# Loads, weight transposes, weight rounding and tables moved into the stages in front of them, in a four-layer network on one core

## The reference, cut to what matters

```
x  = x + attn0(xn) + ffn0(xn)   # causal softmax attention with ALiBi; quantised SiLU feed-forward
x  = x + attn1(xn) + ffn1(xn)   # linear attention with cos/sin features and decay; quantised feed-forward
x  = x + attn2(xn) + ffn2(xn)   # attention with relative position tables; a two-layer local-attention network
x  = x + attn3(xn) + ffn3(xn)   # attention with tied q, k, v; mixture of 8 experts, top 2

def fp4_quant_dequant(x):       # blocks of 16 along the last axis, for activations and for weights
    scale = max(max|x| / 6, 1e-12)
    return nearest_of(0, .5, 1, 1.5, 2, 3, 4, 6)(|x / scale|) * sign(x) * scale
```

## Time and profile before

| what | value |
|---|---|
| median of three runs | 4258.23 us |
| the profiled execution, its own time | 4260.68 us |
| its span | 4258.7 us |
| busy: TensorE, VectorE, ScalarE, GpSimd | 2931.0, 2349.2, 1746.5, 826.7 us |
| granted TensorE clock, mean | 0.783 |

### The profile page before, as it was taken

One profiled execution on the slowest core, in us unless ns is written; L12 is line 12 of the kernel. 1 busy time (PEld: TensorE's weight loads), 2 busy tenths in 40 slices (PEclk: granted clock), 3 DMA queues, 4 the chain that ended last, 5 costly groups with the idle time before them and its releaser, 6 DMA issues. The chain is left out here.

```text
span 4258.7 us, 67695 instructions
## 1 busy us (share of the span) xinstructions
PE 2931.0 (69%) x21547; PEld 1596.1 (37%) x21547; DVE 2349.2 (55%) x4792; ACT 1746.5 (41%) x4244; POOL 826.7 (19%) x1061
## 2 busy tenths in 40 slices
PE   5588846374635787777776687777778722768885
PEld 2344424253423444444443343333333311762221
DVE  4556467454855566666663354444445453138885
ACT  2355511211213455455553244444444401227775
POOL 2100001021113444444441300000000004112220
PEclk9789867686767999999998666666666655889998
DMA  3432110000001000000000577777777615663331
GB/s 113 79 56 52 38 53 0 8 1 6 1 14 48 10 19 18 18 10 18 18 18 3 170 189 196 187 192 192 187 193 192 161 42 158 174 146 55 66 61 37
DMA packets 462309, 340.77 MB, mean 80 GB/s; under 512 B 64351, under 2 KB 424986, under 8 KB 461986
## 3 DMA queue, kind: packets, MB, share of 16 engines
q1 hardware_dynamic: 441474, 308.78, 29.4%
q0 software_dynamic: 8704, 20.99, 1.8%
q10 hardware_dynamic: 11808, 7.08, 0.6%
HBM read 174.71 MB, written 146.81 MB: 75 GB/s over the span
## 5 line engine op out<-in xcount | busy, mean ns | idle before, releaser
L1158 DVE TENSOR_REDUCE a_soft_NM<-a_soft_s_ps 128x2 f32<-128x1024 f32 (+3 forms) x512 | 514.2, 1021 | 204.3 <-PE a_soft_s_ps L1093 132.8
L1192 ACT ACTIVATE a_soft_PTS<-a_soft_st_ps 128x512 f32<-128x512 f32 (+3 forms) x1024 | 458.3, 521 | 147.9 <-PE a_soft_st_ps L1069 101.7
L465 PE MATMUL a_soft_pt_ps<-net_ident,a_soft_PR 128*128 128x128 f32 x1280 | 330.1, 370 | 123.2 <-ACT a_soft_PTS L567 115.8
L613 ACT ACTIVATE a_soft_PR<-a_soft_s_ps,a_soft_least 128x128 f32<-128x128 f32 (+3 forms) x512 | 263.9, 527 | 338.7 <-DVE a_soft_least L588 241.8
L1064 PE MATMUL a_soft_st_ps<-a_soft_QS,a_soft_KS 50*128 50x512 bf16 (+4 forms) x1024 | 257.8, 359 | 60.1 <-ACT a_soft_PTS L1192 32.2
L465 PEld LDWEIGHTS a_soft_pt_ps<-net_ident,a_soft_PR 128*128 128x128 f32 x1280 | 184.1, 181 | 220.8 <-ACT a_soft_PR L613 160.0
L1106 PE MATMUL a_soft_o_ps<-a_soft_PTS,a_soft_VR 128*32 128x512 f32 (+3 forms) x2048 | 240.9, 544 | 0.1
L2275 PE MATMUL f_run_ps<-f_run_WQKV,f_run_HT 128*128 128x512 f32 x384 | 228.9, 687 | 15.2 <-DVE f_run_RS L1496 8.0
L2608 ACT ACTIVATE f_run_PB<-f_run_ps,f_run_MX 128x128 f32<-128x128 f32 x512 | 180.3, 378 | 134.0 <-DVE f_run_MX L2490 134.0
L2413 POOL TENSOR_TENSOR f_run_QK<-f_run_QK,f_run_T 128x512 f32<-128x512 f32 x128 | 163.4, 1277 | 365.6 <-DVE f_run_T L2468 363.2
L569 DVE COPY a_soft_PTS<-a_soft_pt_ps 128x512 f32<-128x512 f32 (+3 forms) x320 | 169.5, 530 | 72.6 <-PE a_soft_pt_ps L465 40.0
(11 more groups left out here) (382 smaller groups left out, 6395.5 us busy)
## 6 DMA issues: line engine op xcount, KB each, us to landing
a_soft_BIAS<-skew_d SPq DMA_DIRECT2D x256, 191.0 KB, 4.3
band_d<-a_soft_PR SPq DMA_DIRECT2D x256, 191.0 KB, 3.8
skew_d<-a_soft_RS SPq DMA_DIRECT2D x128, 256.0 KB, 4.5
a_soft_PB<-band_d SPq DMA_DIRECT2D x128, 256.0 KB, 3.1
f_run_W<-in_L_ffn_w SPq DMA_DIRECT2D x72, 256.0 KB, 2.7
query_rows_d<-a_proj_PARTS SPq DMA_DIRECT2D x96, 128.0 KB, 3.4
key_rows_d<-a_proj_PARTS SPq DMA_DIRECT2D x96, 128.0 KB, 3.8
a_soft_QS<-query_rows_d SPq DMA_DIRECT2D x32, 384.0 KB
```

Of the source, the lines that this page charges most:

```text
L465: last = pe.transpose(pt_ps[:, slot, kb * P:(kb + 1) * P], PR[:, n % NPR, OFF + kb * P:OFF + (kb + 1) * P], ident[:])
L613: act.activation(PR[:, n % NPR, OFF:OFF + width(j)], s_ps[:, n % 4, 0:width(j)], ACT.Exp, bias=least[:, n:n + 1], scale=-1.0).then_inc(pro ...
L1158: dve.tensor_reduce(NM[:, T % 2, j, p, :], s_ps[:, ring["s", a] % 2, :, 0:width(j)], AX.X, ALU.max, negate=True).then_inc(max_ready, 1)
L1192: act.activation(PTS[:, T % 2, 2 * p + par, kb, q0:S], st_ps[:, e % 3, q0:S], ACT.Exp, scale=scale).then_inc(probs_ready, 1)
```

## The change

Preparation is taken out of stages of its own. What it does:

- x is loaded in eight pieces inside n0, with the statistics of each piece behind its load; the identity, a0's weights, masks and biases, the relative tables' rows and the raw weights of both quantised feed-forwards are loaded behind x in the same stage (40 loads). `layernorm_stage` gets loads, transposes (TensorE, ScalarE, in front of the square root) and a first piece of GpSimd work (in front of its copies).
- The six weight matrices are rounded on VectorE inside the attention a0, one of ten instructions every fourth step. `fp4_weights` is gone; the nine blocks of a feed-forward are turned at the start of its own run.
- In f0 the tables of a1 are loaded and the angles computed on GpSimd between batches; the sines and exponentials are made by ScalarE in n1, which also turns a1's weights. GpSimd splits and stacks the relative keys there, with DMAs from its own queue.
- In f1 the weights and tables of f2 are loaded; GpSimd scales the rotary tables between batches. The shift and gain of f2 move to step 14 of its order.
- a2 loads its four weights and two small tables in one stage; n3 takes over the loads, casts and transposes of the last layer.
- The ALiBi rows are written to the query and key tiles from SBUF and no longer through DRAM.

```diff
-def layernorm_stage(nc, stage, X, XN, XNT, ident):
+def layernorm_stage(nc, stage, X, XN, XNT, ident, fill=(), loads=(), turns=(), first_pool=None, first_act=None):
+        @block.sync
+        def _(sp):
+            for b, src in enumerate(fill):
+                sp.dma_start(X[:, TB * b:TB * (b + 1), :], src).then_inc(x_loaded[b], 16)
+            for dst, src in loads:
+                sp.dma_start(dst, src).then_inc(loaded, 16)
+            if loads:
+                sp.wait_ge(loaded, 16 * len(loads))
...
+            for b in range(len(fill)):
+                dve.wait_ge(x_loaded[b], 16)
+                for t in range(TB * b, TB * (b + 1)):
+                    dve.bn_stats(st[:, t, :], X[:, t, :])
...
         @block.scalar
         def _(act):
+            if first_act is not None:
+                first_act(act)
+            for k, (dst, src) in enumerate(turns):
+                a, b = src.shape
+                act.wait_ge(w_turned, k + 1)
+                act.activation(dst, w_ps[0:b, k % 2, 0:a], ACT.Copy).then_inc(w_copied, 1)
             act.wait_ge(var_ready, 1)
             act.activation(rstd[:], var[:], ACT.Sqrt).then_inc(sd_ready, 1)
...
         @block.gpsimd
         def _(pool):
+            if first_pool is not None:
+                if loads:
+                    pool.wait_ge(loaded, 16 * len(loads))
+                first_pool(pool, stored)
             pool.sem_inc(xn_copied, 1)
...
         @block.tensor
         def _(pe):
+            if loads and turns:
+                pe.wait_ge(loaded, 16 * len(loads))
+            for k, (dst, src) in enumerate(turns):
+                ...
+                pe.transpose(w_ps[0:b, k % 2, 0:a], src, ident[0:a, 0:a]).then_inc(w_turned, 1)
...
# turned_attention, VectorE, behind the maxima of a step
+                if matrices and t >= 8 and t % 4 == 0 and (t - 8) // 4 < FP4_STEPS * len(matrices):
+                    dve.drain()
+                    fp4_step(dve, (t - 8) // 4 % FP4_STEPS, matrices[(t - 8) // 4 // FP4_STEPS], QSC[:], QINV[:], QT[:], QM[:])
...
# fp4_ffn, GpSimd
             for b in range(B):
+                if b == 1:
+                    pool.wait_ge(loaded, 16 * len(loads))
+                if b >= 1:
+                    between(pool, b)
                 pool.wait_ge(h_rounded, b + 1)
                 pool.tensor_tensor(HH[:, b % 2, :]..., t[:, b % 2, :]..., bcast(sc[:, b % 2, :], FP4_BLOCK), ALU.mult)
...
# fp4_ffn, TensorE, ahead of turn_x(0)
+            for n in range(3):
+                out = ht_ps[:, n, :] if n < 2 else y_ps[:]
+                for c in range(3):
+                    last = pe.transpose(out[:, c * P:(c + 1) * P], RAW[:, n, c * P:(c + 1) * P], ident[:])
+                last.then_inc(w_turned, 1)
...
+    def angles(self, pool, b):                    # f0, between batches, 128x1024 each
+        if b == 1:
+            for g in range(2):
+                pool.tensor_scalar(ang[:, g, :], self.t["tok_idx"][:], self.t["th"][:, g:g + 1], None, ALU.mult)
+            pool.drain()
+            pool.tensor_scalar(kk[:], ang[:], float(1 / (2 * np.pi)), quarter[:, 0:1], ALU.mult, ALU.add)
+        elif b == 2:
+            pool.tensor_scalar(kk[:], kk[:], ROUND, None, ALU.add)
+            pool.drain()
+            pool.tensor_scalar(kk[:], kk[:], ROUND, None, ALU.subtract)
+        elif b <= 5:
+            step = self.t["TRIG"]
+            pool.tensor_scalar(step[:], kk[:], -TWO_PI[b - 3], None, ALU.mult)
+            pool.drain()
+            pool.tensor_tensor(ang[:], step[:], ang[:], ALU.add)
+        elif b == 6:
+            pool.tensor_scalar(ang[:], ang[:], quarter[:, 1:2], None, ALU.add)
+            pool.drain()
+            pool.tensor_scalar(ang[:], ang[:], 3.1415925, -3.1415925, ALU.min, ALU.max)
+        pool.drain()
...
+    def scaled(self, pool, b, ident, band, SC):   # f1, between batches
+        if b == 1:
+            pool.tensor_scalar(SC[:, :, 0], SC[:, :, 0], 8.0, None, ALU.mult)
+            pool.tensor_copy(self.t["ident_bf"][:], ident[:])
+        elif b <= 5:                              # two products of 128x256
+            ...
+                pool.tensor_tensor(TAB[:, n, k, a], TAB[:, n, k, a], scale, ALU.mult)
+        else:                                     # two copies of 128x256
+            ...
...
+    def stack(self, pool, stored, keys, rest, parts):   # n1
+        split_parts(pool, [parts[:, i, :] for i in range(SPLITS)], rest[:], keys[:])
+        pool.drain()
+        pool.dma_start(self.parts_d.rearrange("(s d) c -> d s c", s=SPLITS), parts[:]).then_inc(stored, 16)
+        pool.wait_ge(stored, 16)
+        ... (six loads of rel_k, and a wait for them)
...
# network
-        load_all(nc, [(X[:], token_tiles(i["L0_attn"]["x"])), (ident[:], cst["ident"])], "load")
-        layernorm_stage(nc, "n0", X, XN, XNT, ident)
-        causal_attention(nc, X, XNT, ident, cst, turned, i["L0_attn"])
-        fp4_layer(nc, "f0", X, XN, ident, i["L0_ffn"], rows_d)
-        layernorm_stage(nc, "n1", X, XN, XNT, ident)
-        linear_layer(nc, X, XNT, ident, cst, i["L1_attn"])
-        fp4_layer(nc, "f1", X, XN, ident, i["L1_ffn"])
...
+                causal_attention(nc, X, XN, XNT, ident, cst, turned, i["L0_attn"], token_tiles(i["L0_attn"]["x"]),
+                                 rel.loads(i["L2_attn"], near, far) + rows(RAW0, "L0_ffn") + rows(RAW1, "L1_ffn"), clear_pads,
+                                 [raw[:, n, :] for raw in (RAW0, RAW1) for n in range(3)])
...
+                    fp4_ffn(nc, "f0_run", X, XN, ident, RAW0, linear.loads(cst, i["L1_attn"]) + [(skew_base[:], cst["skew_base"])], linear.angles,
+                            rows_d, (skew_base[:], rel.skew_d), (keys[:], near[:, 0, :]))
...
+                    layernorm_stage(nc, "n1", X, XN, XNT, ident, turns=linear.turns(), first_pool=stack, first_act=linear.curves)
+                    linear_attention(nc, "a1_run", X, XNT, linear.t, ident)
...
+                    fp4_ffn(nc, "f1_run", X, XN, ident, RAW1, local.loads(cst, i["L2_ffn"], band, SC), scaled)
+                layernorm_stage(nc, "n2", X, XN, XNT, ident)
+                local_network(nc, "f2_run", ..., local.t, RAW1[:].rearrange("p n f -> p (n f)"))
```

More of the change, by code:

```diff
@@ L236, in split_parts, with transpose_weights @@
     return dve.tensor_copy(parts[2], rest)
-def transpose_weights(nc, stage, ident, jobs):
+def transpose_weights(nc, stage, ident, jobs, loads, ones):
     n = len(jobs)
     with Scope(nc, stage) as s:
-        ring = s.sb("ring", [P, 2, P])
-        pt = s.ps("pt", [P, 2, 512])
-        loaded = [s.sem("loaded0"), s.sem("loaded1")]
-        turned, copied = s.sem("turned"), s.sem("copied")
+        ring = s.sb("ring", [P, n, P])
+        pt = s.ps("pt", [P, n, 512])
+        loaded, more_loaded = [s.sem(f"loaded{i}") for i in range(n)], s.sem("more_loaded")
+        turned = s.sem("turned")
         block = s.block()
@@ L1315, in fp4_ffn, with ffn_rows @@
+CH = [(0, P), (P, P), (2 * P, FF - 2 * P)]
+def ffn_rows(RAW, w_gate, w_up, w_down):
+    pairs = []
+    for n, w in enumerate((w_gate, w_up)):
+        pairs += [(RAW[:, n, 0:2 * P].rearrange("p (c f) -> p c f", f=D), w[0:2 * P, :].rearrange("(c p) f -> p c f", p=P)),
+                  (RAW[0:FF - 2 * P, n, 2 * P:3 * P], w[2 * P:FF, :])]
+    return pairs + [(RAW[:, 2, 0:FF], w_down)]
+def fp4_ffn(nc, stage, X, XN, ident, RAW, loads, between, clear=None, skew=None, turn=None):
     NBX, NBH = S // FP4_BLOCK, TB * FF // FP4_BLOCK
@@ L1339, in _ @@
                                    bcast(sc[:, b % 2, :], FP4_BLOCK), ALU.mult).then_inc(hq_ready, 1)
-        if clear is not None:
-            @block.sync
-            def _(sp):
+        @block.sync
+        def _(sp):
+            for dst, src in loads:
+                sp.dma_start(dst, src).then_inc(loaded, 16)
+            sp.wait_ge(loaded, 16 * len(loads))
+            if clear is not None:
                 sp.wait_ge(zeroed, 1)
@@ L1419, in down @@
                 last.then_inc(y_ready, 1)
+            for n in range(3):
[3 more added lines that the diff above has]
+                last.then_inc(w_turned, 1)
+            if turn is not None:
+                rows, r = turn[1], turn[1].shape[1]
+                pe.wait_ge(w_copied, 1)
+                pe.transpose(ht_ps[0:r, 0, 0:P], rows, ident[:]).then_inc(w_turned, 1)
             turn_x(0)
+            pe.wait_ge(w_copied, 3 if turn is None else 4)
             gate_up(0, 0)
@@ L1456, in copy_h @@
                     act.activation(HQT[0:n, c, :], ht_ps[0:n, (3 * b + c) % 2, :], ACT.Copy).then_inc(hqt_ready, 1)
+            for n in range(2):
+                act.wait_ge(w_turned, n + 1)
+                act.activation(WGU[:, n * FF:(n + 1) * FF], ht_ps[:, n, 0:FF], ACT.Copy).then_inc(w_copied, 1)
+            act.wait_ge(w_turned, 3)
+            act.activation(WD[:].rearrange("p c f -> p (c f)"), y_ps[:, 0:3 * P], ACT.Copy).then_inc(w_copied, 1)
+            if turn is not None:
```

(12 more changed lines are left out.)

512 lines of the change are left out of this document (235 added, 277 removed).

## The result

Four runs of the changed kernel took 4093.0 to 4106.3 us, median **4098.63**; four of the kernel before, on the same chip, 4253.2 to 4263.6, median 4257.82. The ratio is 0.9627, 95% interval 0.9607 to 0.9647: 3.7% faster, and the forecast was 4098. The profiled execution took 4106.25 (span 4104.4), 7.6 above its own median.

A forecast was written before the change was run, and what follows sets the result against it. Each working stage has its own bound; preparing stages are serial chains of load, wait and barrier. Gains 188.7 less 3 (shift), 5 (a0) and 20 (GpSimd) give 160.7: 4100 profiled, 4098 median, range 4072 to 4138.

The forecast's parts named there:

- The gains: Preparation removed at the start, f0, f1, a1, f2, a2 and last layer: 15, 32, 32, 41, 35, 23, 10.7 us.
- n0's chain: In n0 all 40 loads land at about 26 us, then turns, square root and GpSimd's piece; ring starts at 32.
- the port's exclusion: In f0 VectorE, the bound, and GpSimd's added table work exclude each other: 14 us lost.
- its first rival: f0 and f1: GpSimd's one-input operations cost twice and block VectorE fully, 37 + 8 instead of 20, 4123 us; chance 0.15.
- its low price: GpSimd's one-input operations of 1024 columns in f0 at 1.2 us each; by the skill's rule 25 us would fall on VectorE.
- f1: mis-sized: In f1 GpSimd's products and copies of 256 columns, 8 us of work, cost VectorE 6 us.
- a0's rounding: In a0 the added VectorE rounding, 25 to 30 us of work, lengthens the stage by 5 us; bounds 0 and 30.
- The rival of the slower side: a0's pieces tear TensorE's stream, its clock stays low: +160, 190 with the pieces' 30, 4283 us; chance 0.02.
- f2's shift: The shift of f2, moved to step 14 while the pipeline fills: 3 of its 6 us count as loss.

The follow-up runs named there:

- experiment 2: The changed kernel without GpSimd's angle work of batches 2 to 6 in f0: 4100.11 us.
- experiment 7: The changed kernel without the rounding of the six weight matrices in a0: 4110.24 us.
- the copies: Tiny ScalarE copies that do nothing, added in n2: 19 or 4 on the changed kernel (ratios 0.9573, 0.9612), 20 on the three edits (0.9515).
- the three edits: Changed kernel with n0's identity on its own semaphore and pieces behind the ring, angle pieces behind x's rounding, GpSimd's two-operation form: 4077.06 us, ratio 0.9552.
- experiment 5: The changed kernel with a second, neutral operation (add 0.0) in GpSimd's one-input operations of the angle work: 4100.53 us.
- a moved wait: The changed kernel with each batch's angle piece waiting until VectorE has rounded x for the next batch: 4084.9 us, ratio 0.9580.

## Why the prediction was right

**The gains were sized right.** 15, 32, 32, 41, 35, 23 and 10.7 were forecast; 15.7, 31.4, 31.9, 41.2, 35.0, 23.4 and 10.7 came, 189.3 for 188.7. Each was read from the last instruction of one working stage to the first of the next, less a barrier of 0.7 and what the code left in the gap. Even n0's chain came out: loads in at 24.7 for 26, ring at 30.3 for 32.

**f0: right in place and size.** 14 was taken for the port's exclusion; experiment 2 gives 13.5. Batches 0 and 7 are equal, as predicted, and batches 1 to 6 are longer by 0.9 to 3.1, where 2 to 3 was forecast for each. The way to it was only half right. The prediction took GpSimd's work in f0 at 17 to 29 us; it is 30 us (5.0, 5.6, three times 5.1 and 3.9 in batches 1 to 6), so the dearer price of its first rival was the right one, or still a little low, and over half of the work hides. What hides is what lies beside reductions, reciprocals and some of the tensor_tensors.

The Trainium skill, "SBUF — State Buffer", section "Who interferes with whom", has the pair as an exclusive lock for the whole instruction, and lets a VectorE operation with two SBUF inputs contend too. The trace agrees in part. The tensor_scalar at 611.76 took 2.43 for 0.43 and ended 0.28 after GpSimd's instruction, but the one at 609.09 took 0.61 for 0.18 and ended at 609.70, while GpSimd's ran on to 611.40: that was no lock for the whole instruction. The tensor_tensor at 609.78 kept its 0.69 beside GpSimd's multiplication alone, with two SBUF inputs; the one at 572.91 took 1.37. The prediction made of this rule that all 25 us of GpSimd's work in f0 and f1, at its low price, would fall on VectorE; 15.5 did.

**f1: mis-sized, 6 for 0.3.** f1's pieces are two products of 256 columns, 1.41 us together, right behind GpSimd's multiply, and batches lengthened by 0.4 at most. What waits there is a tensor_tensor with two SBUF inputs, and no tensor_scalar:

```profile
1007.76 1.41 POOL L2261 TENSOR_TENSOR f_TAB<-f_TAB,f_SC 128x256 f32<-128x256 f32 x2
...
1008.60 1.12 DVE L1291 TENSOR_TENSOR f_run_tx<-net_XN,f_run_invx 128x512 f32<-128x512 f32 x1
```

1.12 for 0.69, in each of batches 2 to 5. The prediction scaled f0's loss by GpSimd's work (8 us here, and it is 8.6); but each piece meets only one operation that waits, and the rest of it lies beside a reduction, a reciprocal or an operation that doesn't wait.

**a0's rounding: 5 for nothing.** VectorE had a third of its time free; experiment 7 bounds the cost within the stretch's scatter. In the changed kernel's profile TensorE was busy as before:

```profile
300.00:400.00 100.00, 85.92 (x1116) 46.10 (x1114) 64.55 (x107) 57.54 (x149) 5.33 (x11) 0.89 0.30 55
```

The rival of the slower side, a torn TensorE stream in a0 with the clock at its lower level, is out: 0.89 for 0.91. (Its price had a slip: 82% of 329 us are 270 and not 246, which by the same factor makes it 175 and not 160.) **f2's shift: 3 for nothing**, f2's run took 1024.0 for 1024.6.

**The step that was missing** is that code which is moved moves the code behind it. The prediction counted engines' time alone and held a2 for untouched. Its heads lost 9 to 22 us over nine profiles, and the copies give back all of it (972.2 to 972.4 in three kernels, 975.5 in the kernel before). Why the place in the program counts is open; that it counts is shown by the copies. It hardly showed in the total because a2's projections were 9.7 shorter and the losses in a0, f1 and f2 14 smaller than allowed: the 4098 is right by luck in this part.

**What stays open** is a2's projections. They took 62.7 to 64.0 in seven profiles and 73.0 to 76.0 in the seven others, among them both of the kernel before, and the two kernels that were profiled twice each repeated their own value, as did the three edits. It goes with the granted clock. In slices of 8 us it was 0.71, 0.79 and from there 1.00 in the second profile of the changed kernel; in the one without rounding it stayed between 0.50 and 0.79, with TensorE busy all the time in both.

The two ways part before the stage. In experiment 5 and in the second profile of the changed kernel f2 runs alike within 0.1 us for 970 us; then, 53 to 55 us ahead of the projections, the same 32 products meet the clock at different levels, granted 0.50 and 1.00. First experiment 5, then the changed kernel:

```profile
2146.32 1.99 PE L2347 MATMUL f_run_ps<-f_run_KT,f_run_QT 64*64 64x128 f32 x32
```
```profile
2151.39 1.10 PE L2347 MATMUL f_run_ps<-f_run_KT,f_run_QT 64*64 64x128 f32 x32
```

From there on f2 ends 2.7 later, the same 2.7 as in experiments 2 and 7, and the projections take 12 more. What sets the clock at that point I can't tell: edits of GpSimd's form or of a0's rounding change it, and so do the copies in the changed kernel, though not in the one with three edits; a moved wait does not. No run tested it. It is worth 12 us either way, more than most of the edits here, and it makes medians of single kernels misleading: experiments 2, 5 and 7 look slower than the changed kernel mainly for it.

a0's projections do much the same between executions of one kernel: 56.8 and 63.65 before. The granted clock of TensorE in the kernel before, first profile, and then in the changed one (stretch, length, TensorE busy, clock, DMA share, GB/s):

```profile
80.00:88.00 8.00, 8.00 (x25) 0.71 0.79 235
88.00:96.00 8.00, 8.00 (x35) 0.99 0.80 248
```
```profile
80.00:88.00 8.00, 8.00 (x25) 0.75 0.84 253
88.00:96.00 8.00, 8.00 (x28) 0.79 0.78 238
```

Equally busy, but in the first it stayed at the upper of the two levels (1.2 and 2.4 GHz) from 88 on, and in the other it went on changing between them.

## What to carry to other kernels

Cut both spans at the stages' first instructions and compare term by term, even where the total agrees: here a miss of 22 us hid behind luck of the same size. When work goes to GpSimd beside a VectorE that bounds the stage, look at which VectorE operations it will meet, and put it beside reductions and reciprocals, which never waited here; a two-input operation waits beside some of GpSimd's operations, so read it from a profile. And give each consumer a semaphore of its own: one gate for all loads, with the pieces behind it in front of the ring, cost 11 us at the start of a kernel whose edits were meant to take waits away.

## What the runs showed of the hardware that was not expected

- Beside a GpSimd instruction VectorE's tensor_scalar of 512 columns took up to 2.43 us for 0.43; reductions (0.68, 1.62) and reciprocals (0.35, 0.70) ran as always. f2's scalar_tensor_tensor waits as well.
- VectorE's tensor_tensor of 512 columns with two SBUF inputs kept its 0.69 us beside GpSimd's multiplication alone or addition alone, and took up to 1.37 beside its multiplication with addition (one of the two that met it, the other 0.69) and 1.12 beside its tensor_tensor.
- GpSimd's tensor_scalar on 1024 float32 columns: multiplication alone 2.77 us, addition alone 2.79 to 2.85, minimum with maximum 1.04 to 1.39, multiplication with addition 1.04 to 1.67, addition with addition 3.66 to 3.80, subtraction with addition 3.63 to 4.05 (all beside some VectorE work).
- The place of a loop in an engine's program counts. ScalarE's idle time at the turn of a loop of 335 instructions was 5.2 to 7.9 us with the loop at instruction 2151 or 2166, 8.4 to 10.7 at 2147, and at 2146 6.4 to 8.4 with another 1.7 to 2.7 behind the first operation.
- 24 equal products at the end of f1 took 5.49 us or 2.94, by the clock that TensorE had been granted.
